# A gated recurrent attention block with a ternary feed-forward network: the last residual put on by an adding DMA, x1 in three buffers, the loop's lists in another order

## The reference

```
x = x + tanh(g_xattn) * recurrent(layernorm(x), ctx)
x = x + tanh(g_ffn)   * ffn(layernorm(x))

recurrent, one step for each of the 128 positions:
    r = decay * r + k * v                    # k = v = ctx
    inp = (q * r) @ Wi.T + bi
    gate = sigmoid(inp @ Wg.T + bg)
    blended = gate * state + (1 - gate) * inp
    state = tanh(blended @ A.T + inp @ Bm.T)
    out = state @ Wo.T + bo

ffn:  relu(x @ Wq1.T + b1) @ Wq2.T + b2      # Wq1, Wq2 rounded to -1, 0, 1
```

## Time and profile before

| | |
|---|---|
| median of 3 runs | 324.3 us (323.25 to 327.12) |
| the profiled execution | 323.17 us |
| its span, first to last instruction | 321.4 us |
| busy, share of the span | TensorE 93%, VectorE 88%, ScalarE 73%, GpSimd 35% |
| granted clock of TensorE, mean | 0.994 |

### The profile page before, as it was taken

The page is one execution under the profiler, slowest core; times in us unless marked ns, Lnnn a source line. Parts: engine busy times, 40 slices in busy tenths (PEclk is TensorE's granted clock), DMA queues, the critical chain, the costliest instruction groups (busy, mean ns, idle before and its releaser), DMA issues.

```text
span 321.4 us, 9314 instructions
## 1 busy us (share of the span) xinstructions
PE 297.8 (93%) x3550; PEld 261.0 (81%) x3550; DVE 282.6 (88%) x915; ACT 235.6 (73%) x561; POOL 114.0 (35%) x233
## 2 busy tenths in 40 slices
PE   7989688999999999999999999999999999998895
PEld 5767477788898989798888989897988889886684
DVE  5876999999999999999999999999999999969763
ACT  3687557877878786868778787868787786866584
POOL 3653044270605234161706153351607061502130
PEclk9999899999999999999999999999999999999999
DMA  8945016125253515344253525153442333260321
GB/s 271 398 107 147 31 37 128 36 36 141 55 134 63 128 42 98 103 66 133 35 138 64 131 57 122 57 83 114 64 137 36 66 68 67 57 111 0 67 33 67
DMA packets 19852, 29.97 MB, mean 93 GB/s; under 512 B 1888, under 2 KB 10336, under 8 KB 19680
## 3 DMA queue, kind: packets, MB, share of 16 engines
q0 software_dynamic: 8864, 8.65, 19.0%
q1 hardware_dynamic: 10512, 20.19, 18.9%
q10 hardware_dynamic: 432, 0.53, 0.5%
HBM read 16.52 MB, written 4.19 MB: 64 GB/s over the span
## 4 chain that ended last, share of the span: by engine, by line
PE 69%; DVE 11%; ACT 11%; issue 5%; POOL 2%; DMA 1%; ACTq 0%; DVEq 0%; POOLq 0%
PE y_ps L1307 13%; PE hid_ps L1293 11%; PE inp_ps L1213 9%; PE att_ps L1265 6%; PE pre_ps L1165 6%; PE pre_ps L1245 6%; PE ret_ps L1186 5%; ACT inp L500 4%; PE pre_ps L1251 4%; ACT inp_hi L506 3%; PE ret_ps L1195 2%; PE ret_ps L1176 2%; PE att_ps L1274 2%; DVE h_lo L892 1%; DMA cols<-cols_in 1%
## 5 line engine op out<-in xcount | busy, mean ns | idle before, releaser
L567 ACT ACTIVATE state<-pre_ps,tanh_unit 128x64 f32<-128x64 f32 x120 | 37.4, 312 | 41.3 <-PE pre_ps L1251 41.0
L1307 PE MATMUL y_ps<-w_q,h_hi 128*128 128x256 bf16 x240 | 58.3, 274 | 0.7 <-DVE h_lo L892 0.7
L1307 PE MATMUL y_ps<-w_q,h_lo 128*128 128x256 bf16 x240 | 57.8, 272 | 0.0
L557 ACT ACTIVATE hid<-hid_ps,b_s 128x256 f32<-128x256 f32 x120 | 50.2, 473 | 9.5 <-PE hid_ps L1293 9.5
L1293 PE MATMUL hid_ps<-xt_lo,w_q 128*128 128x256 f16 x240 | 54.8, 272 | 0.0
L1293 PE MATMUL hid_ps<-xt_hi,w_q 128*128 128x256 f16 x240 | 54.8, 272 | 0.0
L1245 PE MATMUL pre_ps<-m_hi,a_hi 128*128 128x32 f16 x508 | 42.2, 178 | 6.8 <-DVE m_hi L827 4.8
L384 POOL TENSOR_TENSOR bi_unit<-cols,unit 128x2 f32<-128x2 f32 x15 | 2.8, 186 | 128.2 <-DVE unit L847 128.2
L1245 PEld LDWEIGHTS pre_ps<-m_hi,a_hi 128*128 128x128 f16 x508 | 36.0, 96 | 13.1 <-DVE m_hi L827 8.3
L1245 PE MATMUL pre_ps<-m_hi,a_lo 128*128 128x32 f16 x508 | 41.5, 176 | 0.0
L821 DVE SCALAR_TENSOR_TENSOR mix<-state,unit,inp 128x64 f32<-128x64 f32 x120 | 33.2, 277 | 9.4 <-ACT state L567 7.1
(11 more groups left out here) (215 smaller groups left out, 841.2 us busy)
## 6 DMA issues: line engine op xcount, KB each, us to landing
x_norm<-x_rows_in SPq DMA_DIRECT2D x16, 256.0 KB, 3.4
cx<-ctx_in SPq DMA_DIRECT2D x16, 256.0 KB, 3.3
x_res<-x_in SPq DMA_DIRECT2D x16, 256.0 KB, 2.6
x_res<-bo_g POOLq DMA_DIRECT2D x16, 256.0 KB, 3.8
x<-b_g POOLq DMA_DIRECT2D x15, 256.0 KB, 3.8
y_out<-y SPq DMA_DIRECT2D x15, 256.0 KB, 2.0
w_raw<-w_in SPq DMA_DIRECT2D x2, 512.0 KB, 7.1
w_raw<-w_in SPq DMA_DIRECT2D x1, 1024.0 KB, 9.7
```

Source lines behind the costliest of these rows:

```text
L557: last = nc.scalar.activation(hid[:, p % 2, u, :], hid_ps[p % 2][:, u * N:(u + 1) * N], ACT.Relu, bias=b1_s[:, 2 * p + u:2 * p + u + 1], s ...
L567: nc.scalar.activation(state[:, q[1] % 2, :, step_cols(j)], pre_ps[q[1] % 2][:, :].rearrange("p (k n) -> p k n", k=K)[:, :, step_cols(j)], ...
L1307: last = nc.tensor.matmul(y_ps[:, t * D:(t + 1) * D], h[:, f, t * P:(t + 1) * P], w2_q[:, f, :], start=f == 0 and t == 0 and h is h_hi, st ...
```

## The change

- `finish` is no longer called in the loop's bodies for chunks 0 to 12. In its place ScalarE writes y as `y_ps` times the gate (`y_out`), behind tanh 1, and GpSimd then issues an adding DMA that puts x1 onto y (`add_x1`). `finish` stays for chunks 13 and 14, `end_finish` for the last.
- The store waits for that DMA (`x1_added`) instead of `y_set`, up to chunk 12.
- x1 has three buffers instead of two. `residual` waits for the adding DMA of three chunks back instead of for `finish` of two back.
- `from_inp` waits for `inp_lo_set` once more.
- The lists of all four engines are put in another order. Among others: on TensorE hidden 0 stands ahead of step 0, both input products between steps 1 and 2, `bound_product` behind y 3, and only y 7 behind step 7; on ScalarE `inp_out` stands behind tanh 2, hidden 2 and 3 between tanh 3 and 4, `carry` ahead of `norm_apply`; on VectorE the residual comes in slot 1, `norm_mean` behind step 5, `scan` behind step 7; on GpSimd `bound_of` and `add_x1` come first and `add_b2` between `rstd1_of` and `shift1_of`.

```
-        x1 = sb("x1", [P, 2, TILES, D])
+        x1 = sb("x1", [P, 3, TILES, D])
...
             def store(q):
-                sp.wait_ge(y_set, upto(q))
+                sp.wait_ge(*((x1_added[q[1] % 2], landed(q)) if q[1] < NC - 3 else (y_set, upto(q))))
...
+            def add_x1(q):
+                pool.wait_ge(y_set, upto(q))
+                pool.wait_ge(b2_added[q[1] % 2], landed(q))
+                pool.dma_start(y[:, q[1] % 2, :, :], x1[:, q[1] % 3, :, :],
+                               accum_op=ALU.add).then_inc(x1_added[q[1] % 2], 16)
...
+                if norm:
+                    bound_of(norm)
+                if exists(plus(c, -3)):
+                    add_x1(plus(c, -3))
                 if project:
                     scales_of(project)
                 if attend:
                     rstd2_of(attend)
+                if norm:
+                    rstd1_of(norm)
+                if attend:
                     add_b2(attend)
                 if norm:
-                    bound_of(norm)
-                    rstd1_of(norm)
                     shift1_of(norm)
...
+            def y_out(q):
+                if exists(plus(q, -2)):
+                    act.wait_ge(stored[q[1] % 2], landed(plus(q, -2)))
+                act.wait_ge(y_sum, upto(q))
+                nc.scalar.mul(y[:, q[1] % 2, :, :], y_ps[:, :].rearrange("p (t d) -> p t d", t=TILES),
+                              gate_sc[:, 1:2]).then_inc(y_set, 1)
...
             def residual(q):
-                if exists(plus(q, -2)):
-                    dve.wait_ge(y_set, upto(plus(q, -2)))
+                if exists(plus(q, -3)):
+                    dve.wait_ge(x1_added[(q[1] - 3) % 2], landed(plus(q, -3)))
...
             def from_inp(q, m):
+                pe.wait_ge(inp_lo_set, upto(q))
```

More of the change, by code:

```diff
@@ L663, in body @@
                     state_high(attend)
+                if project:
+                    bound_out(project)
+                if ffn:
+                    hidden(ffn, 0)
                 if chain:
@@ L666, in body @@
                 if ffn:
[L667 removed]
                     hidden_high(ffn, 0)
[L669 to L670 removed]
+                    hidden(ffn, 1)
+                if norm:
+                    square(norm)
                 if peeled == 1:
@@ L674, in body @@
                     tanh_step(chain, 1)
+                if exists(plus(c, -3)):
+                    y_out(plus(c, -3))
                 if ffn:
[L676 to L679, removed]
+                    hidden_high(ffn, 1)
                 if peeled == 1:
@@ L685, in body @@
                     tanh_step(chain, 2)
-                if ffn:
-                    hidden_high(ffn, 1)
-                    hidden(ffn, 2)
+                if project:
+                    inp_out(project, 0)
+                    inp_out(project, 1)
                 if peeled == 1:
@@ L693, in body @@
                 if ffn:
+                    hidden(ffn, 2)
+                if project:
+                    inp_high(project)
+                if ffn:
                     hidden_high(ffn, 2)
[L695 to L698, removed]
+                    hidden(ffn, 3)
                 if peeled == 2:
@@ L705, in body @@
                 if ffn:
-                    hidden(ffn, 3)
                     hidden_high(ffn, 3)
+                if attend:
+                    normed_high(attend)
                 if peeled == 1:
@@ L718, in body @@
                 if norm:
+                    carry(project)
                     norm_apply(norm)
@@ L1077, in body @@
                     norm_stats(norm)
+                if attend:
+                    residual(attend)
                 if peeled == 1:
@@ L1083, in body @@
                     gated_state(chain, 2)
+                if attend:
+                    x1_stats(attend)
                 if ffn:
                     hidden_low(ffn, 0)
-                if attend:
-                    residual(attend)
                 if chain:
                     gated_state(chain, 3)
[L1090 to L1095, removed]
                 if attend:
                     x1_mean(attend)
+                if ffn:
+                    hidden_low(ffn, 1)
                 if peeled == 1:
@@ L1113, in body @@
                     hidden_low(ffn, 2)
+                if chain:
+                    gated_state(chain, 5)
+                if ffn:
+                    hidden_low(ffn, 3)
+                if norm:
+                    norm_mean(norm)
                 if peeled == 1:
@@ L1121, in body @@
                     gated_state(chain, 6)
+                if attend:
+                    normed_low(attend)
+                if chain:
+                    gated_state(chain, 7)
                 if norm:
                     scan(norm)
-                if chain:
-                    gated_state(chain, 7)
-                if ffn:
-                    hidden_low(ffn, 3)
-                if attend:
-                    normed_low(attend)
                 if peeled == 1:
@@ L1421, in body @@
                 if ffn:
-                    hidden_product(ffn, 0)
                     hidden_product(ffn, 1)
-                if chain:
-                    step(chain, 1)
                 if attend:
@@ L1428, in body @@
                     output_product(attend, 1)
+                if chain:
+                    step(chain, 1)
+                if project:
+                    inp_product(project, 0)
+                    inp_product(project, 1)
+                if chain:
+                    step(chain, 2)
                 if ffn:
                     hidden_product(ffn, 2)
-                if chain:
-                    step(chain, 2)
-                if project:
-                    inp_product(project, 0)
-                if ffn:
-                    y_product(ffn, 0)
+                    hidden_product(ffn, 3)
                 if peeled == 1:
```

59 lines of the change are left out of this document (26 added, 33 removed).

## The result

The changed kernel takes 328.5 us (median of 20 runs, 327.45 to 331.91) against 324.3 for the kernel before beside it: 1.013 times as long, with a 95% interval of 1.010 to 1.016. It was forecast at 315.1. So a change that takes 0.66 us of work a body off VectorE makes the kernel slower. The profiled execution took 328.45, its span is 326.7.

The account below looks back on a forecast made before the run. VectorE's queue was taken as the bound, nearly 17.5 of 17.73 us a body. Twelve bodies at 0.6 (7.2) and 0.85 in the tail, taken from 323.17, gave 315.1; range 312.5 to 330.5.

Parts of the forecast that it names:

- rival 1: GpSimd's shift falls behind VectorE's scan, delaying `norm_apply` and tanh 7: +0.6 to +0.8 a body, about 330 us; chance 0.32.
- GpSimd's order (b): On GpSimd after `norm_mean` at 13.05, shift begins between 15.2 and 15.6, scan at 15.5; if through, body 17.05 to 17.2.
- the prediction's own limit: Rival 1 decides once GpSimd's shift begins 2.5 us after `norm_mean`'s end; summed as 2.2 or 2.5 to 2.6.
- The margin: Between GpSimd's shift and VectorE's scan: called smaller than the prediction's error.
- The lock: A VectorE operation with two SBUF inputs and a GpSimd operation reading SBUF exclude each other for the whole instruction.
- The timetable: `mix` starts through a body, laid slot by slot over VectorE, TensorE and ScalarE: body 17.05 us, 0.68 less.
- The handover: `y_out` on ScalarE 0.69, covered; `add_x1` holds GpSimd 0.82 or 1.23; third x1 buffer and later store cost nothing.
- The bound before: VectorE's own queue, nearly 17.5 of 17.73 us a body; TensorE close behind at 16.7 to 16.8.
- The ends: Bodies 1 and 2 stay; the tail's first hidden comes about 0.85 us earlier.
- Rival 2: Relief eaten where three full engines meet: body 17.4 to 17.6, 319.3 us with 317 to 322 around it; chance 0.18.

Follow-up runs that it names:

- b2 in one piece: The changed kernel with gated b2 kept twice side by side, so the b2 add reads one run of 512 elements a partition: 313.9 us.
- the new lists alone: The changed kernel with `finish` back on VectorE behind step 0 and no adding DMA of x1: 333.1 us.
- the b2 add earlier: The changed kernel with the b2 add one place up in GpSimd's list, directly behind `rstd2_of`: 313.0 us.
- the handover in the old lists: The kernel before with `y_out` behind tanh 0, `add_x1` first in GpSimd's body and three x1 buffers, otherwise old order: 321.9 us.

## Why the prediction was wrong

What came is its rival 1, in mechanism and place; its price, 329 to 331.5, was a little high (the profiled execution took 328.45), since a body lost 0.55 where 0.6 to 0.8 was given. By its steps:

- **The step that failed** is the last of "GpSimd's order (b)": shift begins "between 15.2 and 15.6", the scan at 15.5, and of the two ends of that span the lower was taken as the likelier. The term that was mis-sized is what an issue holds of GpSimd's queue. It was carried as 0.82 or 1.23, 0.82 being the distance to the *start* of the next instruction. On the chip the next instruction starts 0.80 after the issue, and isn't done until 0.23 after the issue's end: `off` at 161.28 + 0.66 = 161.94 against 160.48 + 1.23 = 161.71. The same 0.23 to 0.24 stands behind `add_x1` (`bi_unit` ends at 152.63, the issue at 152.40) and in the run with b2 in one piece (157.24 and 157.00). From the issue to the end of `off` that is 1.46, where 0.82 and 0.2 to 0.3 were taken. So 1.23 was the price, the shift came 2.55 after the end of `norm_mean` (159.47), and the prediction's own limit was 2.5. The start of an instruction behind an issue was read as the issue's end.
- **The margin.** It was called smaller than the error, and that was right: over the two kernels in which the shift met the scan it was decided between 14 and 19 ns. No row of before could have settled that to the ns. Which of 0.82 and 1.23 to take, its trace did say. In body 14 and the next three issues follow one another on GpSimd:

```profile
278.29 1.23 POOL L419 DMA_DIRECT2D x<-b_g  x1 [1.49 <-DVE xh L879]
279.08 2.92 POOL L427 DMA_DIRECT2D x_res<-bo_g  x2
```

From 278.29 to 282.00 they take 1.24 each, though the second row begins 0.79 after the first. So the larger hold should have had the larger chance. In the run of the new lists alone a body was 1.15 shorter when the shift got through; by that an estimate for the changed kernel is 18.27 - 1.15 = 17.12. A few ns more of lead would have brought the forecast's body by luck, with the same term mis-sized.
- **The lock.** The Trainium skill, page "SBUF — State Buffer", section "SBUF: two separate sides", was cited for the exclusion of a VectorE operation with two SBUF inputs and a GpSimd operation that reads SBUF. The runs agree that the one holds the other for its whole length (1.35 for 1.35). It says that the one which starts first gets through; by the profile's start times a lead of 1 to 14 ns was not enough (162.02 against 162.03, 110.40 against 110.41), one of 19 or 20 was (129.32 against 129.34). The other way round the runs don't show a hold of whole length: there the shift's row covers the scan's first 0.18, and the scan grew by 0.03.
- **The timetable** was right up to step 7: forecast 1.8, 4.7, 6.9, 8.55, 11.3, 13.0, 14.65, measured 1.79, 4.68, 6.92, 8.56, 11.32, 12.96, 14.72. With the shift free the body is 16.82 to 16.83, 0.2 under the forecast's 17.05: it comes down to the sum of TensorE's pieces (16.7 to 16.8), with next to nothing lost between the engines. (One sum of the timetable is off by 0.05: TensorE's slots add up to 16.7 and not 16.75. It changes nothing.)
- **The handover** costs what was said: `y_out` is 0.68 long (0.69 forecast), and the tanh behind it waits 0.72 for TensorE, so it is covered. `scales_of` behind the adding DMA is late (0.50 for `bi_unit`), yet `inp` at 152.80 begins right behind its tanh at 152.44. The third buffer and the store cost nothing that shows.
- **The bound before** was read too narrowly. VectorE was called the bound and TensorE put at 16.7 to 16.8; the 0.6 a body for which TensorE stood waiting for `inp_high` was not added, and the page's chain that ended last, 69% TensorE and 11% VectorE, was not weighed. With that wait both engines were nearly full, and the handover alone was worth 0.17 a body. It did little harm to the forecast, since with the new lists that wait is gone.
- **The ends.** Bodies 1 and 2 were said to stay; together they are 1.1 longer in the changed kernel. Body 14 and the tail give back 2.4, of which body 15 takes 0.4 again, where 0.6 for body 14 and 0.85 for the tail were forecast. What makes these sizes was not tested. They are not the shift's: with the b2 add earlier bodies 1 and 2 are together 1.1 longer too, and body 14 and the tail 2.4 shorter. The shorter end comes with the new lists (2.2 with them and `finish` on VectorE, shift free); of the longer start, the handover in the old lists shows 1.0 as well, in body 1.
- **Rival 2**, the relief eaten where full engines meet, fits the old lists (0.17 of 0.66 came through) and not the new ones (0.62).

## What to carry to other kernels

When an order is changed, put the small operations of a side engine on the same clock as the large ones, and where a 0.2 us operation comes nearer to a long operation that can lock it out than the error of the estimate (here 0.4, the distance between the two prices of one issue), count it as lost, with everything that waits behind it; or move it by a place rather than hope. Read an engine's hold from when the next operation *ends*. And before an engine is relieved, add to every other engine's work the waits that stand in its own list: they can be as much a floor as its instructions.

## What the runs showed of the hardware

- The issue of an adding DMA holds GpSimd for the whole length of its row, though the next instruction's row begins 0.25 to 0.43 before that row's end: in nearly all bodies the operation of 128x2 behind it, 0.19 long by itself, ends 0.23 or 0.24 after that end (161.94 against 161.71). The Trainium skill, page "Perfetto Trace Analysis", section "DMA Instruction — SWDGE (GPSIMD)", ends such a row where the last descriptor is written, not where the data have moved. The rows agree with the second part: the 256 KB land 3.3 to 4.9 (medians of the lines in these runs) after the start of an issue of 0.89 to 1.70. What the row's end marks, no row here shows.
- That length goes by runs: for 256 KB it is 0.89 to 0.90 with one run of 512 elements a partition, and 1.23 with one of 256 read twice; 128 KB in one run of 256 are 0.89 as well. The median to landing fell with it, from 3.8 to 3.4. Two issues of 1.23 back to back come one after the other: the second is 1.70 long, from 0.79 after the first one's start to 2.49 after it.
- GpSimd and the scan: with a recorded lead of 1 to 14 ns GpSimd's 128x2 operation took 1.34 to 1.35 instead of 0.20, with the scan unchanged at 1.35; with 19 or 20 ns the operation took 0.20 and the scan 1.38.
